# Cross attention with 64-row score products, two heads stacked in one tile

## The reference

```python
# B=8, S=512, D=256, 16 heads of 16
q = split_heads(layernorm(x) @ Wq.T + bq)
k = split_heads(ctx @ Wk.T + bk)
v = split_heads(ctx @ Wv.T + bv)
scores = einsum('bhqd,bhkd->bhqk', q, k) / sqrt(16)
scores = where(mask == 0, -1e9, scores)      # this mask is all ones
attn = softmax(scores, axis=-1)
x = x + merge_heads(einsum('bhqk,bhkd->bhqd', attn, v)) @ Wo.T + bo
```

## Time and profile before

| | before |
|---|---|
| median of three runs | 2753.31 us |
| the profiled execution's own time | 2755.81 us |
| its span | 2754.1 us |
| mean granted TensorE clock | 0.942 of full |
| PE busy | 2213.0 us (80%), 11991 matmul instructions |
| DVE busy | 1623.1 us (59%) |
| ACT busy | 912.9 us (33%) |
| POOL busy | 913.8 us (33%) |
| DMA | 254.24 MB, mean 92 GB/s |

### The profile page before, as it was taken

The page is one execution under the profiler, slowest core; times in us unless marked ns, Lnnn a source line. Parts: engine busy times, 40 slices in busy tenths (PEclk is TensorE's granted clock), DMA queues, the critical chain, the costliest instruction groups (busy, mean ns, idle before and its releaser), DMA issues. The chain is left out here.

```text
span 2754.1 us, 37523 instructions
## 1 busy us (share of the span) xinstructions
PE 2213.0 (80%) x11991; PEld 1495.9 (54%) x12000; DVE 1623.1 (59%) x2734; ACT 912.9 (33%) x1265; POOL 913.8 (33%) x778
## 2 busy tenths in 40 slices
PE   2430999999999106989899999756999999999998
PEld 1330999999999102444444444453554555555554
DVE  7720455445554453778777778653666666566565
ACT  2410333433333000445544445321233333233332
POOL 0076455424450631233322333200323323333232
PEclk9999999999999556999999999859999999999998
DMA  3252332333322316465565565523333233223322
GB/s 122 91 215 96 115 118 67 120 119 122 107 73 76 118 55 116 71 108 97 89 96 93 97 108 98 90 73 81 74 77 77 62 77 84 66 66 84 77 54 61
DMA packets 150695, 254.24 MB, mean 92 GB/s; under 512 B 19318, under 2 KB 68350, under 8 KB 148322
## 3 DMA queue, kind: packets, MB, share of 16 engines
q1 hardware_dynamic: 110858, 173.08, 28.9%
q0 software_dynamic: 11104, 44.06, 4.7%
q10 hardware_dynamic: 28688, 36.53, 4.1%
HBM read 130.05 MB, written 67.04 MB: 72 GB/s over the span
## 5 line engine op out<-in xcount | busy, mean ns | idle before, releaser
L1084 DVE TENSOR_REDUCE ca_negmax<-ca_na 128x1 f32<-128x512 f32 x544 | 353.3, 676 | 135.7 <-PE ca_na L874 133.2
L997 ACT ACTIVATE ca_pr<-ca_st 128x1024 f32<-128x1024 f32 x256 | 261.2, 1024 | 290.8 <-PE ca_st L888 290.6
L874 PE MATMUL ca_na<-ca_k_stack,ca_q_stack 128*128 128x512 f32 x544 | 241.8, 450 | 54.2 <-DMA ca_q_stack<-ca_zrow 37.0
L592 DVE TENSOR_TENSOR ex_h<-ex_up,ex_sg 128x512 f32<-128x512 f32 x136 | 94.1, 692 | 305.5 <-ACT ex_sg L555 197.8
L888 PE MATMUL ca_st<-ca_q_stack,ca_k_stack 128*128 128x512 f32 x512 | 269.6, 527 | 0.0
L1688 DVE TENSOR_REDUCE sa_negmax<-sa_na 128x1 f32<-128x512 f32 x272 | 182.6, 674 | 131.1 <-PE sa_na L1509 127.0
L515 PE MATMUL ex_gp<-ex_xp,moe_gu_p 128*128 128x256 f32 x1632 | 221.8, 286 | 1.5 <-DVE ex_xp L578 1.4
L528 PE MATMUL ex_yp<-moe_dn_p,ex_hp 128*128 128x256 f32 x1632 | 209.0, 286 | 11.9 <-DVE ex_hp L582 11.9
L515 PE MATMUL ex_up<-ex_xp,moe_gu_p 128*128 128x256 f32 x1632 | 218.5, 283 | 0.0
L1676 POOL TENSOR_TENSOR sa_acc<-sa_acc,sa_pr 128x1024 f32<-128x1024 f32 x64 | 151.4, 2365 | 170.4 <-ACT sa_pr L1627 170.4
L528 PEld LDWEIGHTS ex_yp<-moe_dn_p,ex_hp 128*128 128x128 f32 x1632 | 198.8, 191 | 15.9 <-DVE ex_hp L582 15.9
(11 more groups left out here) (258 smaller groups left out, 4191.2 us busy)
## 6 DMA issues: line engine op xcount, KB each, us to landing
ca_q_stack<-q_parts SPq DMA_DIRECT2D x144, 128.0 KB
ca_k_stack<-k_parts SPq DMA_DIRECT2D x144, 128.0 KB
sa_q<-sa_qh SPq DMA_DIRECT2D x140, 128.0 KB
sa_k<-sa_kh SPq DMA_DIRECT2D x140, 128.0 KB
ex_raw_m<-masks ACTq DMA_DIRECT2D x34, 512.0 KB, 3.7
moe_gu_raw<-gateupT POOLq DMA_DIRECT2D x8, 2048.0 KB, 8.2
expert_rows<-rt_zeros SPq DMA_DIRECT2D x20, 512.0 KB, 15.7
k_parts<-ca_kp SPq DMA_DIRECT2D x9, 1024.0 KB, 7.3
```

Source lines behind the costliest of these rows:

```text
L592: dve.tensor_tensor(h[:, 2 * q:2 * q + 2, :], up[q % 2][:, :, :], sg[:, q % 2, :, :], ALU.mult).then_inc(h_ready, 1)
L874: pe.matmul(na[s % 2][:, :], q_stack[g][:, h, t * P:(t + 1) * P], k_stack[g][:, h, :], start=not masked, stop=True).then_inc(na_full, 1)
L997: act.activation(pr[:, pair // 2 % 2, h:h + 2, :], st[pair % 2][:, :, :], ACT.Exp, scale=DK ** -0.5).then_inc(exp_done, 1)
L1084: dve.tensor_reduce(negmax[:, g % 2, s % TB, s // TB:s // TB + 1], na[s % 2][:, :], AX.X, ALU.max, negate=True).then_inc(max_done, 1)
```

## The change

One stack of 128 partitions now holds two heads above each other: partitions 0 to 63 one head, 64 to 127 the next (j = 0, 1). In each half 48 rows hold three products (the low x low product is gone), two rows the maximum, and 14 rows zeros against ones. A stack's middle index shrinks from 4 to 2. Each score matmul takes 64 rows. `score_b` of slot s uses half s % 2, `score_a` of slot s the other half, 1 - s % 2. A group takes 14 DMAs: twelve of 16 partitions x 2 x 512 and two that clear maximum rows. The maxima of a unit are laid out so that one transpose gives 16 rows of 128; ACT's copy and POOL's split work on 16 x 128, and four DMAs instead of two send the rows. The set-up covers all 128 partitions of the half as long stacks.

```diff
-        R4 = 4 * DK
+        HALF, RM = P // 2, 3 * DK
...
-        q_stack = [m.sb(f"q_stack{g}", [P, HG, S], F32R) for g in range(G)]
-        k_stack = [m.sb(f"k_stack{g}", [P, HG, S], F32R) for g in range(G)]
-        negmax = m.sb("negmax", [P, 2, TB, HG])
-        zrow = m.sb("zrow", [2, P])
-        mfull, mrow = m.sb("mfull", [HG, S]), m.sb("mrow", [HG, 2, S], F32R)
+        q_stack = [m.sb(f"q_stack{g}", [P, HG // 2, S], F32R) for g in range(G)]
+        k_stack = [m.sb(f"k_stack{g}", [P, HG // 2, S], F32R) for g in range(G)]
+        negmax = m.sb("negmax", [P, 2, 2, 2, TB])
+        zrow = m.sb("zrow", [2, S])
+        mfull, mrow = m.sb("mfull", [HG * TB, P]), m.sb("mrow", [HG * TB, 2, P], F32R)
...
-                for r in range(4):
-                    for stack, dram, part in ((q_stack[g], q_parts, r % 2), (k_stack[g], k_parts, r // 2)):
-                        sp.dma_start(stack[r * DK:(r + 1) * DK, :, :].bitcast(F32),
-                                     dram[part, h, :].rearrange("(h d) n -> d h n", d=DK)).then_inc(stack_in[g], 16)
-                sp.dma_start(q_stack[g][R4:R4 + 2, :, :].bitcast(F32).rearrange("p h (t n) -> p (h t) n", n=P),
-                             zrow[:, :].rearrange("p (a n) -> p a n", a=1).to_broadcast([2, HG * TB, P])).then_inc(stack_in[g], 16)
+                for j in range(2):
+                    for r in range(3):
+                        lo = j * HALF + r * DK
+                        for stack, dram, part in ((q_stack[g], q_parts, r % 2), (k_stack[g], k_parts, r // 2)):
+                            sp.dma_start(stack[lo:lo + DK, :, :].bitcast(F32),
+                                         dram[part, h, :].rearrange("(i j d) n -> j d i n", j=2, d=DK)[j]).then_inc(stack_in[g], 16)
+                    lo = j * HALF + RM
+                    sp.dma_start(q_stack[g][lo:lo + 2, :, :].bitcast(F32),
+                                 zrow[:, :].rearrange("p (a n) -> p a n", a=1).to_broadcast([2, HG // 2, S])).then_inc(stack_in[g], 16)
...
-                for t in range(TB):
-                    last = pe.transpose(misc[0:HG, t * P:(t + 1) * P], negmax[:, par, t, :], ident[:, :])
-                last.then_inc(misc_full, 1)
+                pe.transpose(misc[0:HG * TB, 0:P], negmax[:, par, :, :, :].rearrange("p j i t -> p (j i t)"), ident[:, :]).then_inc(misc_full, 1)
...
-                h, t = s // TB, s % TB
+                t, i, rows = s // 2 % TB, s // (2 * TB), slice((1 - s % 2) * HALF, (2 - s % 2) * HALF)
...
-                pe.matmul(na[s % 2][:, :], q_stack[g][:, h, t * P:(t + 1) * P], k_stack[g][:, h, :],
+                pe.matmul(na[s % 2][:, :], q_stack[g][rows, i, t * P:(t + 1) * P], k_stack[g][rows, i, :],
                           start=not masked, stop=True).then_inc(na_full, 1)
...
-                t, h = s // HG, s % HG
+                t, i, rows = s // HG, s % HG // 2, slice(s % 2 * HALF, (s % 2 + 1) * HALF)
...
-                last = pe.matmul(out, k_stack[g][:, h, t * P:(t + 1) * P], q_stack[g][:, h, :], start=not masked, stop=True)
+                last = pe.matmul(out, k_stack[g][rows, i, t * P:(t + 1) * P], q_stack[g][rows, i, :], start=not masked, stop=True)
...
-                    act.copy(mfull[:, :], misc[0:HG, :]).then_inc(misc_free, 1)
+                    act.copy(mfull[:, :], misc[0:HG * TB, 0:P]).then_inc(misc_free, 1)
...
                 for r in range(2):
-                    act.dma_start(q_stack[g][R4 + r:R4 + r + 1, :, :].bitcast(F32), mrow[:, r, :].bitcast(F32)).then_inc(m_in, 16)
+                    for j in range(2):
+                        row = j * HALF + RM + r
+                        act.dma_start(q_stack[g][row:row + 1, :, :].bitcast(F32).rearrange("a i (t n) -> a (i t) n", n=P),
+                                      mrow[j * 2 * TB:(j + 1) * 2 * TB, r, :].bitcast(F32)).then_inc(m_in, 16)
...
-                dve.memset(k_stack[g][R4:P, :, :].bitcast(F32), 1.0).then_inc(set_up, 1)
-                dve.memset(q_stack[g][R4:P, :, :].bitcast(F32), 0.0).then_inc(set_up, 1)
+                dve.memset(k_stack[g][:, :, :].bitcast(F32), 1.0).then_inc(set_up, 1)
+                dve.memset(q_stack[g][:, :, :].bitcast(F32), 0.0).then_inc(set_up, 1)
```

More of the change, by code:

```diff
@@ L730, in cross_attention @@
         SETUP = 6 + 2 * G
-        LOAD = 16 * 9
+        LOAD = 16 * 14
         SLOTS = TB * HG
@@ L873, in score_a @@
                     pe.matmul(na[s % 2][:, :], ident16[:, :], nb[:, b % 2, t, :], start=True, stop=False)
-                pe.matmul(na[s % 2][:, :], q_stack[g][:, h, t * P:(t + 1) * P], k_stack[g][:, h, :],
+                pe.matmul(na[s % 2][:, :], q_stack[g][rows, i, t * P:(t + 1) * P], k_stack[g][rows, i, :],
                           start=not masked, stop=True).then_inc(na_full, 1)
             def score_b(g, b, s, u, masked):
-                t, h = s // HG, s % HG
+                t, i, rows = s // HG, s % HG // 2, slice(s % 2 * HALF, (s % 2 + 1) * HALF)
                 pair = s // 2
                 if s == 0:
-                    pe.wait_ge(m_in, u * 32 + 32)
+                    pe.wait_ge(m_in, u * 64 + 64)
                 if s % 2 == 0:
@@ L1002, in _ @@
             take(B * G)
-            act.wait_ge(m_in, 32 * (B * G + 1))
+            act.wait_ge(m_in, 64 * (B * G + 1))
         @block.gpsimd
@@ L1021, in split_rows @@
                 if not (isinstance(a, int) and a == 0):
-                    pool.wait_ge(m_in, a * 32)
-                pool.tensor_tensor(mrow[:, 0, :].rearrange("p (t n) -> p t n", n=P), mfull[:, :].rearrange("p (t n) -> p t n", n=P),
-                                   ones[0:HG, :].rearrange("p (a n) -> p a n", a=1).to_broadcast([HG, TB, P]), ALU.mult).then_inc(mh_ready, 1)
+                    pool.wait_ge(m_in, a * 64)
+                pool.tensor_tensor(mrow[:, 0, :], mfull[:, :], ones[0:HG * TB, :], ALU.mult).then_inc(mh_ready, 1)
                 pool.wait_ge(mh_ready, a + 1)
@@ L1083, in maximum @@
                 dve.wait_ge(na_full, a * SLOTS + s + 1)
-                dve.tensor_reduce(negmax[:, g % 2, s % TB, s // TB:s // TB + 1], na[s % 2][:, :], AX.X, ALU.max,
+                dve.tensor_reduce(negmax[:, g % 2, 1 - s % 2, s // (2 * TB), s // 2 % TB:s // 2 % TB + 1], na[s % 2][:, :], AX.X, ALU.max,
                                   negate=True).then_inc(max_done, 1)
```

## The result

The whole change takes **2702.38 us** (median of 4 runs, 2698.11 to 2708.74); the kernel before, run beside it, took 2752.73 us. The ratio is 0.9821, 95% interval [0.9803, 0.9838]: 1.8% faster, 7 us slower than the forecast of 2695 and inside its range. The sum came out nearly right, but several of its terms were wrong, in opposite directions, as the following shows.

The account below looks back on a forecast made before the run. Limits differed by unit: PE and DVE nearly tied in 0, PE in 1, the stack wait in 2, DVE in 3. Terms gave -6.3 us a batch, -50 in the loop, -58 with set-up: median 2695 us, range 2660 to 2760.

Parts of the forecast that it names:

- step 1: Each slot's two score matmuls run at once, saving 0.23 us a slot, 3.7 us a unit on PE.
- rival A: Score halves don't run side by side: +10 us in the loop less 7.5, about 2756, no change; chance 0.13.
- step 2: Tile-shape changes around 128-row pieces cost 0.28 us each: 2.2, 2.2, 2.0, 0.3 us in units 0 to 3.
- step 3: Maxima: one transpose instead of four saves PE 0.25 us per unit; ACT's two extra DMAs stay hidden.
- step 4: Stack loads of group 0 to `score_a` take 9.3 us instead of 11.74, -2.4 us.
- the sum for unit 0: PE's own path shrinks by 1.7 us, bounded by DVE's busy 18.2; -1.6 us taken.
- step 5: Set-up before PE's first projection: -6.5 us; with -1 from the first stack load, -7.5, once.
- Rival B: The clock falls in units 2 and 3 as scores overlap and PE stands more: 2777 us, slower; chance 0.13.
- The unit windows I named: Predicted lengths of units 0 to 3: 20.5, 21.0, 19.4 (wait of 2 us within) and 15.1 us.

Follow-up runs that it names:

- the three terms: Kernel before with three products, one head per stack, seven 128 KB loads, full-height matmuls, and set-up fills moved into VectorE's gaps: 2685.24 us; with 16-row maxima 2680.05.

## Why the prediction was right in sum and wrong in steps

1. **Scores (step 1): the mechanism right, counted in too many slots.** The scores run side by side, so rival A fell, and the overlap is worth 0.22 us in a slot with a piece (forecast 0.23). I counted 16 slots in each of units 0 and 1. Of unit 1's, eight have a piece, four a group of `values`, and four are bare. By the starts of `score_b` (medians over the batches; full-height scores with three terms, fills in the gaps and 16-row maxima, then the whole change), slots 4 to 6, two bare ones and one with a piece, take 3.02 and 3.00 us, with PE waiting for a maximum in slot 6 in both: nothing is gained. Slots 10 and 11 take 2.22 and 1.66. So a bare slot paid only where PE waited for no maximum behind it. From the first score to the piece behind it the two take 0.66 us on one half and 0.43 on two. The Trainium skill (TensorEngine Tiling, Theoretical Speedup) puts the gain at up to 2x. These two spans differ by 1.5x.
2. **Borders (step 2): mis-sized.** 0.39 us a slot with a piece (1.72 against 1.33), forecast 0.28. With the overlap's 0.22 that leaves +0.17 for each such slot (1.50 against 1.33), where I had +0.05. The ruler has, for interval 1-2, +2.0 us for half-height scores on the same half against full-height ones (22.73, 20.73) and -1.4 for the two halves (21.33): +0.6 together, where I had -1.5 for unit 1. Over a batch the change costs 1.04 us against full-height scores with the same terms and maxima (77.15 against 76.11), 8 us in the loop; PE waits for loads 0.4 us in all there and not at all here, but the size and number of the loads differ too.
3. **Maxima (step 3): mis-sized.** 0.4 us a batch where it was measured, on the three terms, not 1.0. That ACT's two more transfers are hidden held: no row shows `score_b` waiting for the maximum rows in the loop.
4. **Loads (step 4): right, and the wait went altogether.** I had 9.3 us; from first issue to `score_a` lie 9.26 us, and PE does not wait for the data, so it took less. From q1's evacuation to `score_a` 17.16 instead of 19.85, the evacuation 5.58 into the unit instead of 6.43: 3.5 us, more than the wait of 3.0. I kept 2 us of wait because PE's own path was to shrink by 1.7, and it did not. So unit 1's missing gain appears as unit 2's: 16.93 us, where I had 17.0 behind the wait plus 2 of wait. The same loads also took away unit 0's wait for `nbT`, which the sum for unit 0 did not count (7.7 us in the loop before, none now).
5. **Set-up (step 5): mis-sized.** -11.7 instead of -6.5. I halved the duration only. Each fill of 2048 columns leaves 0.38 us idle behind it (2.14 from start to start), one of 1024 columns 0.16 (1.07), and the first three here begin while the cast still runs.
6. **The clock.** I had its fall behind unit 2's wait stay; it went with the wait. Rival B, given 0.13, came in part: the clock was low from slot 2 or slot 15 of unit 3 on, in six of eight batches of one profile and four of the other, for 10.9 and 9.0 us. Its reason was not as I wrote it, since no longer wait of PE stands there. All four profiles with half-height scores had a loop clock below 1.00 (0.96 to 0.99); the full-height ones without a wait had 1.00. The Trainium skill (TensorE: Matmul & The Clock Gate, HAM oscillation) ties the falls to idle gaps. The rows show the fall with PE's records covering 3.65 of the 4 us ahead (3.1 to 3.3 of 4 for the falls in slot 15), and with gaps of 0.83 us at most. What in the half-height stream brings it on stays open.

Forecast: -50 in the loop, -7.5 in the set-up. Measured: -43 by the steps, +11 by the clock, -12.7 up to the loop, and some -7 of scatter in the profile, which the medians (-50.4) have only in part. That the median came within 7 us of the forecast is partly luck: the set-up gave 5 us more than I had, the steps of the loop 7 less, and the clock took 11 that I had not. The unit windows I named also add up to -6.1 us a batch, not the -6.3 of the sum; unit 2's should have been 19.2.

## What to carry to other kernels

Try the part that shortens a transfer by itself before the part that re-tiles the matrix engine: here seven loads instead of nine brought more in the loop than the whole change. Half-height matmuls here gained 0.22 us by overlap and lost 0.39 by the change of height in each slot with a full-height piece, so count both, slot by slot, and count nothing for slots that another engine paces. And see that a control run takes away what it is to take away: with both scores of a slot on one half, the overlap only moved to the next slot where no piece stood between. And fills that only a later load needs belong in the idle gaps behind the first evacuations.

## What the runs showed that I had not expected

- A slot of two scores and a full-height piece: 1.33 us with full-height scores, 1.72 with half-height ones on one half, 1.50 on two. In such a slot, going back and forth costs more than running side by side saves.
- A DMA share of 0.96 and one of 0.36 can belong to rates of 126 and 103 GB/s. At 64 KB an issue a piece of 2 KB took 165 ns on average in one loop and 99 in another.
- DVE's normalisations take 7.16 us beside GpSimd's fills and 1.38 without; the cast of a 128 x 128 tile at the block's start takes 3.55 us in the same neighbourhood.
- A later fill on DVE leaves idle time that goes with its length: 0.38 us at 2048 columns, 0.16 at 1024.
- The clock fell with no idle gap of TensorE over 0.83 us in the 14 us ahead of it, always in slot 2 or 15 of unit 3, and did so only with half-height scores.
